# Two transformer stacks in one program: another set of products issued in halves, and fewer quartered products in the first tiles

## The reference

```
x = X
x = x + retention(layernorm(x))          # one head, xpos rotation, softmax, decay mask
x = x + stack(layernorm(x))              # 6 layers, see below
x = x + mixer(layernorm(x))              # RWKV-like mixer with a scan over time
x = x + stack(layernorm(x))              # the same 6 layers and weights again

def stack(x):
    for i in range(6):
        x = attention(shift_tokens(x), Wqkv[i], q_scale[i], k_scale[i], Wo[i]) + x
        x = ffn(shift_tokens(x), ln_g[i], ln_b[i], W1[i], b1[i], W2[i], b2[i]) + x
    return x
```

## Time and profile before

| what | value |
|---|---|
| median of 3 runs | 3589.45 us |
| lowest and highest of them | 3568.89 and 3592.11 us |
| the profiled execution: its own time | 3608.3 us |
| its span, first to last instruction | 3606.2 us |
| mean granted TensorE clock in it | 0.965 |
| DMA packets of the queue "q8 instruction" | 493, 8.08 MB |

### The profile page before, as it was taken

How to read it: one execution, slowest core, us unless ns; L and a number is a source line. 1 busy time by engine, 2 the same in 40 slices (tenths; PEclk the granted TensorE clock), 3 DMA queues, 4 the chain that set the end, 5 groups by cost and what they waited for, 6 DMA issues and landing times. The chain is left out here.

```text
span 3606.2 us, 155076 instructions
## 1 busy us (share of the span) xinstructions
PE 3381.6 (94%) x61984; PEld 2523.7 (70%) x61984; DVE 3344.1 (93%) x11899; ACT 2043.2 (57%) x3659; POOL 2704.4 (75%) x2440
## 2 busy tenths in 40 slices
PE   6799999999999999988699689999999999999997
PEld 4677777777777777763466467777777777777775
DVE  6899999999999999955799799999999999999994
ACT  2456666666666666644422145666656666666663
POOL 1688888888888888843144288888888888888882
PEclk9799999999999999988799689999999999999999
DMA  1233333333333332320000123333333333333332
GB/s 44 57 90 83 76 90 77 92 78 82 92 81 81 86 83 67 76 59 17 0 1 1 36 50 90 80 77 91 71 91 71 85 88 84 75 92 75 75 70 66
DMA packets 151820, 250.65 MB, mean 70 GB/s; under 512 B 42688, under 2 KB 73408, under 8 KB 150976
## 3 DMA queue, kind: packets, MB, share of 16 engines
q1 hardware_dynamic: 151104, 240.75, 27.8%
HBM read 38.21 MB, written 1.05 MB: 11 GB/s over the span
## 5 line engine op out<-in xcount | busy, mean ns | idle before, releaser
L619 PE MATMUL stack_work<-stack_w_qkv,stack_xst 128*128 128x256 f32 (+2 forms) x3760 | 1182.3, 444 | 20.9 <-ACT stack_sq L898 15.7
L1354 POOL TENSOR_TENSOR stack_roped<-stack_rot_c,stack_rot_s 128x512 f32<-128x512 f32 x768 | 979.2, 1287 | 236.9 <-PE stack_work L629 118.0
L1364 POOL TENSOR_TENSOR stack_roped<-stack_roped,stack_rnorm 128x512 f32<-128x512 f32 x768 | 790.5, 1043 | 159.5 <-DVE stack_rnorm L1131 159.5
L898 ACT ACTIVATE stack_sq<-stack_work 128x512 f32<-128x512 f32 x768 | 456.9, 595 | 716.4 <-DVE stack_rot_s L1099 712.2
L619 PEld LDWEIGHTS stack_work<-stack_w_qkv,stack_xst 128*128 128x128 f32 x3760 | 656.0, 197 | 147.4 <-issue 39.8
L1097 DVE TENSOR_TENSOR stack_rot_c<-stack_work,rot_tables 128x512 f32<-128x512 f32 x768 | 516.0, 672 | 36.4 <-PE stack_work L619 33.5
L1099 DVE TENSOR_TENSOR stack_rot_s<-stack_work,rot_tables 128x512 f32<-128x512 f32 x768 | 518.6, 675 | 0.0
L1108 DVE TENSOR_REDUCE stack_ssq<-stack_sq 128x8 f32<-128x512 f32 x768 | 512.2, 672 | 3.3
L1142 DVE CUSTOM_DVE_ANT_0 stack_s_m<-stack_bank_s,band 128x64 f32<-128x64 f32 x3072 | 468.7, 214 | 15.0 <-PE stack_bank_s L644 11.7
L629 PE MATMUL stack_work<-ident,stack_roped 128*128 128x128 f32 x3072 | 437.3, 279 | 15.6 <-ACT stack_sq L898 8.8
L1380 POOL TENSOR_TENSOR stack_s_m<-stack_s_m,stack_inv 128x512 f32<-128x512 f32 x384 | 412.0, 1073 | 22.4 <-DVE stack_inv L1160 22.4
(11 more groups left out here) (255 smaller groups left out, 5093.5 us busy)
## 6 DMA issues: line engine op xcount, KB each, us to landing
stack_v_even<-stack_v_nat SPq DMA_DIRECT2D x768, 128.0 KB, 2.4
stack_p_pairs<-stack_p_turned SPq DMA_DIRECT2D x1536, 64.0 KB
stack_w_qkv<-table_ffn_qkv SPq DMA_DIRECT2D x192, 96.0 KB
stack_w_o<-table_ffn_wo SPq DMA_DIRECT2D x12, 512.0 KB, 4.0
stack_w<-table_ffn_w SPq DMA_DIRECT2D x12, 384.0 KB
stack_w<-table_ffn_w SPq DMA_DIRECT2D x12, 192.0 KB
x_outer<-L_attn_a_X SPq DMA_DIRECT2D x4, 256.0 KB, 7.4
ret_xpos<-table_xpos SPq DMA_DIRECT2D x1, 1024.0 KB, 6.8
```

What stands on the lines that cost most here:

```text
L619: last = pe.matmul(bank[:, s], xst[:, g.row, P * T:P * (T + 1)], w_qkv[:, g.half, col:col + 512 // pieces], start=True, stop=True)
L898: act.activation(sq[:, i % 2, :], work[(BANK["p_" + c][T] + g.row) % 4][:, :], ACT.Square).then_inc(done["squared_" + c], 1)
L1354: pool.tensor_tensor(roped[:, i, T % 2, :], rot_c[:, i % 2, :], rot_s[:, i % 2, :], ALU.add).then_inc(done["roped_" + c], 1)
L1364: pool.tensor_tensor(r, r, rnorm[:, T % 2, i, :].unsqueeze(2).broadcast_to([P, 8, HD]), ALU.mult).then_inc(done["united_" + c], 1)
```

## The change

The set HALVED has 17 entries before and 17 after, of which 8 are common. QUARTERED goes from 25 to 21 for stack 0 and stays 17 for stack 1. Nothing is computed otherwise, and no other engine's instructions change.

```
 HALVED = {
-    ("gate", 1), ("gate", 2), ("k0", 1), ("k0", 2), ("k0", 3), ("k1", 0),
-    ("k1", 1), ("lin", 0), ("lin", 1), ("q0", 1), ("q0", 3), ("q1", 0),
-    ("q1", 2), ("v0", 1), ("v1", 1), ("v1", 2), ("v1", 3),
+    ("center", 0), ("gate", 1), ("k0", 0), ("k0", 1), ("k0", 3), ("k1", 3),
+    ("lin", 0), ("lin", 2), ("q0", 2), ("q0", 3), ("q1", 1), ("v0", 0),
+    ("v0", 1), ("v0", 2), ("v1", 2), ("v1", 3), ("variance", 0),
 }
-QUARTERED = (25, 17)
+QUARTERED = (21, 17)
```

## The result

The changed kernel takes 3629.95 us (median of 4 runs, 3619.49 to 3634.32) against 3588.91 us (4 runs, 3568.89 to 3592.11). The ratio is 1.0099, 95% interval 1.0075 to 1.0124. The forecast was 3576 us. The profiled execution took 3629.42 us, with a span of 3627.6 us and a mean granted clock of 0.965, as before. Note that the profiled executions differ by 21 us (3608.3 and 3629.4) and the medians by 41, since the profiled one of before was slower than every timed one of its runs.

What follows compares the result with a forecast made beforehand. TensorE and VectorE were taken as both near full (94% and 93%), advancing in step. Terms 3 + 8 + 0 + 2 = 13 us less took 3608.3 to 3595, scaled to 3576 us; range 3545 to 3630 us, forecast band 3565 to 3585.

Steps and rivals of the forecast that it cites:

- (b): `weigh` stalls of 1.2 to 1.7 us with slow clock behind, 15.5 us on DVE: shrink to 0.7 us, 8 us gained.
- the block without a term: Block of slot T=2 that ends in scores: listed as 4.7 us long, with no gain or loss assigned.
- rival 1: Slower, late packets in the new short blocks with `weigh`: 3685 us in full (chance 0.06), 3630 us in part (0.11).
- places A and B: Block cuts that move: A from near the end of scores into `down`, B from `project_out` to the slot's end.
- (a): Scores stall, 13.3 us of PE, gone with the 3.0 us block; worth 0 to 13.3 us, taken as 3 us.
- (c): New 4.3 us block in place A: next code there at 7.2 us, needed at 8.2, no stall; taken as 0.
- (d): First and last tiles, whose block lengths change: 5 us lost to 6 gained, taken as 2 us gained.
- Pieces at no cost: Whole and halved products take 0.86 us each; cost of the new pieces bounded at 0 to 3 us, taken as 0.
- The signs that I named: Right: PE's scores wait falls from 13.3 below 4 us; rival 1: `weigh` <- issue over 30 us, steady clock under 0.99.

Runs made afterwards that it cites:

- run 4: The changed kernel with QUARTERED = (25, 17), the old number for the first tiles: 3583.88 us, 0.9969 of the kernel before.
- run 3: The changed kernel with 56 idle semaphore increments ahead of TensorE's first wait in the retention phase: 3571.08 us, 0.9938 of the kernel before.
- run 8: The changed kernel with QUARTERED = (26, 17) in place of (21, 17), without increments: 3575.11 us, 0.9961 of the kernel before.
- run 9: The changed kernel without SyncE's copies of values and probabilities from layer 1 on, so weighing reads old data: 3600.85 us, 1.0030 of the kernel before.
- the table: Seven kernels: before; before with QUARTERED (21, 17), 1.0065; changed, 1.0099; changed with (26, 17), 0.9961, without copies, 1.0030, with 16 or 32 TensorE increments, 1.0058, 1.0015.
- run 5: The changed kernel with 12 idle increments on SyncE ahead of its eight copies of the probabilities in every fourth tile: 3623.81 us, 1.0091 of the kernel before.
- run 6: As run 5, with 24 idle increments on SyncE ahead of the four copies of values in every fourth tile too: 3636.77 us, 1.0123 of the kernel before.

## Why the prediction was wrong

- **The sign was wrong:** 13 us less was forecast, and the kernel took 41 us more.
- **Where it failed, first: the step (b),** "the stall shrinks to 0.7 us, which the slack of a group covers". It took the packet's start as fixed 6 us after the old beginning in the few groups that stall, and named "more groups may see such a stall" without a price. After the change the block begins where large products are all that lies ahead of `weigh`. Its packet started early in 14 of 40 groups and with `weigh` in 22. From there it needs its 1.1 us and some 1.4 us more, against 229 instructions that last 1.8 us. So each late packet costs about 1 us, and there were 27 such gaps in place of 9. The term was 8 us of gain; on TensorE it is 27 us of gaps against 11.4, so some 16 us lost, and on DVE 19.7 us of idle time behind them against 13.8, so 6 us lost.
- **Where it failed, second and for more: the block without a term.** The prediction lists "4.7 us for one with 211 of scores" among the short ones and gives it no term, since a packet within 1.8 us of its beginning was enough for it. Before, all 40 packets of this place started within 1.5 us. After, 14 came over 3 us late, and they made 26.5 us of gaps and, with the clock behind them, 29.8 us of idle time of DVE that was not there before. The mechanism was rival 1's, a packet that starts late in a short block; I had looked for it in places A and B only, and gave it 17 in 100. Its partial price, 3630 us, happens to be the time measured; that is luck, since it was reckoned for other blocks.
- **(a) held in place.** The scores' gap of place A is gone. What that was worth alone no run isolates: run 4 has 36 gaps of about 0.5 us in scores in the whole program, 19 us of its 41, and is 0.3% faster than the kernel before.
- **(c) held.** The 4.3 us block in place A has 9 gaps, 6.4 us, in the whole program, and most of that in the first and last tiles.
- **(d)** was sized at 2 us of gain and measured 6.5.
- **A reading:** the block of place A begins at 779.67, not at 780.10; its packet, at 781.06, was 1.4 us late and not 0.9. Nothing in the sum hangs on it.
- **Pieces at no cost held:** runs 3 and 8 have the new pieces and are faster than the kernel before.
- **The signs that I named** did their work: `weigh` <- issue was to be over 30 us for rival 1 and was 23.0, the scores' wait was to fall below 4 and was 21.9, at another place than the one it had left. The sign of rival 1 was set for two places in `weigh` and missed one in scores.
- **The cause that I gave for late packets,** SyncE's copies at 56.5 and 60% of the DMA engines, was not the cause in one of the places (run 9: late on idle queues, and in more groups) and a part of it in the other. The Trainium skill, "Runtime: NRT & Kernel Launch", Instruction fetch mechanics, calls the cost of a boundary "mostly hidden". The runs agree for most of the ten blocks of a group, and not for the other two or three: where those begin moved the kernel between 0.9938 (run 3) and 1.0099 of its time.

**Open.** What decides, in one group, whether the packet starts at once or only some 3 to 6 us later was not found; that late ones follow a separate wait is seen, not explained. Nor does the length of the large products decide it: in run 8 they last 6.98 us, the longest of the table, and all 40 packets are early. For the block of T=2 there is a strong correlation: over nine kernels (the table's, with runs 5 and 6, 40 groups each) its packet was over 3 us late in 55 of the 63 cases in which the block began within 1.65 us of the previous packet's landing, and in 20 of the other 297. So a late packet seems to make the next one late. In run 9 only one block there began so soon, which would explain why leaving out the copies helped in T=2 and not in T=0: without them the packets ahead land sooner. For the block that ends in T=0, which begins some 5 us after the previous landing, this says nothing; there, in the changed kernel, 15 of the 18 groups in which TensorE had passed its last wait 0.57 us or more ahead of the block's first load had a late packet, and 8 of the 22 others. Both limits were chosen after looking, and no run changed one of these alone.

## What to carry to other kernels

In an unrolled kernel that keeps TensorE over 90% busy, an edit that adds or removes a few instructions shifts every later code boundary, and this alone moved the time between 0.994 and 1.010 here, so an edit's own worth is known only after its boundaries are shifted too. Count 256 instructions at a time and look at each block in which long products come first and a run of short ones (scores, `weigh`) ends it. Its packet may start only 3 to 6 us after the block began, and what is left of the block must then last 2.3 to 3.2 us, the time from a packet's start to the first instruction behind the gap in the stalls shown here. The cure is as cheap as the harm: a few instructions in the first tiles, as in run 8.

## What the runs showed of the hardware that was not expected

- A code packet can start 3.6 us after its block begins although no DMA queue moves anything in that time (run 9), and then within 0.1 us of the first of the short instructions. Packets over 3 us late start mostly (467 of 615) 0.9 to 1.5 us behind the latest separate wait of TensorE, in one block of the kernel before while large products still run for 2.3 us.
- A packet can also start before its block's first instruction is executed (by 0.9 us on average in run 4), so a block of 1.35 us stalls for about 0.5 us only.
- While a code packet moves, SyncE's issue of a copy takes up to 1.93 us (row of run 5) in place of 0.59. In the changed kernel, from 150 us on, 37% of the 494 issues that overlapped a code packet took over 1.2 us, and none of the 2,034 others.
- A gap of 2.22 us on TensorE brought 3.4 us at a granted clock of 0.56; the gap of 1.08 us in `weigh` brought none (1.00 in the 4 us behind it).
- 204 increments of a semaphore on TensorE cost 24 us at the start, 0.12 us each; 56 of them cost 1.4 us and 16 next to nothing (first work at 9.5 and 8.2 us in place of 8.1), since there they ran while the first loads were still under way.
